# A routed expert stage on one core: the second accumulator folded into the output, the order of experts known sooner, and the smallest experts in the middle places

## The chip, the cores and the metric

The kernel runs on one core of one Trainium2 chip. The metric is the device time of one launch in microseconds (us). Lower is better.

## What is computed

One transformer layer over 2048 tokens of 256 numbers, in float32: a layer norm, attention with 16 heads (a band of 32 tokens back, and 16 global tokens), a residual, a second layer norm, and a feed-forward part that is the sum of two things: a shared SwiGLU over all tokens, and 64 experts of which each token uses 6. The change touches only the feed-forward part:

```python
scores = softmax(x @ gate_w.T)
topk_w, topk_idx = top_k(scores, 6)              # 64 experts, 6 per token
topk_w = topk_w / topk_w.sum(-1, keepdims=True)
# per expert e, for the tokens routed to it:
eo = (silu(buf @ w_gate[e].T) * (buf @ w_up[e].T)) @ w_down[e].T
y[token] += eo * topk_w                          # six additions per token
out = x1 + y + silu(x @ sh_gate.T) * (x @ sh_up.T) @ sh_down.T
```

`x1` is what attention and the residuals leave; it stays in SBUF in the tile `X1`, 16 blocks of 128 tokens.

## The kernel before, in words

**Attention and routing.** For every block of 128 tokens the kernel computes attention, then the router's choice, and GpSimd (POOL) scatters the block's rows with their six choices and weights into a DRAM array `expert_rows` by indirect DMAs, six of 128 rows per block (L1836). Meanwhile, TensorE (PE) goes on with the shared SwiGLU, two blocks at a time ("pairs" 0 to 4; pair_gate is L786, pair_up L797, pair_down L811). Blocks 0 and 1 are done earlier, and the last four blocks (NTL = 4, pairs 5 and 6) are left for after the experts.

**The order of the experts.** Between pairs 3 and 4 the counts per expert are turned into ranks on VectorE (DVE, function `ranks`). PE multiplies two small matrices by the one-hot rank matrix (L928, L929, at the head of pair 4), and DVE (`order`) writes `ids` (which expert stands in which place), `by_rank`, and `crowded` (how far an expert exceeds its room). The four experts 0 to 3 are FIXED in places 0 to 3; the other places follow by falling count. `HALF` (L73, from `LEVELS`, L71) gives for each place how many rows each of two tiles of this expert has: 128 for the first places, 72 for the last. `moved` rounds it up to a multiple of 16 for DMAs.

**The experts.** Each engine then runs 64 steps. For expert e: SP (SyncE) loads its rows, `XG` (L478), and its weights (L469 to L471: 368, 128 and 48 KB; 12 weight buffers, so 12 experts ahead, some of them in tiles that are free now: XB, zero, SMX, VW). PE transposes the rows (L947), multiplies (L960, L964), and multiplies down (L978, L981). ScalarE (ACT) does the SiLU (L1220, L1222) and scales the result into one of four `YE` buffers (L1233). DVE copies and multiplies (L1635, L1644, L1652) and computes from the rows each token's weight and address (`choices`, L1621 to L1625). POOL adds the two tiles of YE to DRAM by indirect DMAs with accumulation (L1850): even places into `acc_a`, odd ones into `acc_b`. The adds of place e wait until those of place e-2 have landed; ACT and DVE wait for those of place e-4 (YE has four buffers).

**Two programs.** If an expert is more crowded than its room, another version with loops runs (`full > 0`); the graded version that runs here stands in the `Else` on all five engines, and the closing part stands behind both.

**The end.** Once the adds are in, acc_a is loaded to SBUF in four quarters (L1903, POOL's queue), acc_b in four more (L566, SP's queue, after the last add has landed), both are added to X1 by DVE (L1690, L1697) and POOL (L1890, L1899), the shared SwiGLU of the last four blocks is added (pair_add, L1509), and SP stores out in four quarters (L569).

**SP's order before the experts:** wait `routed` (all rows scattered), load XG for places 0 to 3, wait `order_ready`, load the weights of places 4 to 11, read `crowded`, branch, and only then load XG for place 4 (L478 from L555).

Of the kernel before, what the change touches and what calls it, by code (L numbers as in the profile page):

```python
# [18 lines left out]

# [53 lines left out]
HALF = [P] * FIXED + [h for n, h in LEVELS for _ in range(n)]  # L73
# [40 lines left out]
def build(nc, x, glob, ln_s, ln_b, wq, wk, wv, wo, gate, w1, w2, shg, shu, shd, out):  # L114
    rows = nc.dram_tensor("expert_rows", (EX * CAP, ROW), F32, kind="Internal").ap()
    acc_a = nc.dram_tensor("acc_a", (T, D), F32, kind="Internal").ap()
    acc_b = nc.dram_tensor("acc_b", (T, D), F32, kind="Internal").ap()

    with ExitStack() as ctx:
# [61 lines left out]
        XA = SMX[:, :].rearrange("p (t d) -> p t d", t=NT)  # L181
# [29 lines left out]
        room = sb("room", [1, EX])  # L211
        count_e = sb("count_e", [EX, 1])
# [92 lines left out]
        a_ready, b_ready = sem("a_ready"), sem("b_ready")  # L305
# [10 lines left out]
        b_closed = sem("b_closed")  # L316
        a_in, b_in = sem2("a_in", 4), sem2("b_in", 4)
        a2_added = sem("a2_added")
        a_added, out_stored = sem("a_added"), sem("out_stored")
        sum_ready = sem2("sum_ready", 4)  # L320
# [106 lines left out]
        def quarter(v, q):  # L427
            return v[0:T, :].rearrange("(p t) d -> p t d", p=P)[:, q * NQ:(q + 1) * NQ, :]

        def held(v, q):  # L430
            return v[:, q * NQ:(q + 1) * NQ, :]
# [17 lines left out]
        def _(sp):  # L449
# [36 lines left out]
            def step(s):  # L486
# [14 lines left out]
                if s == 2 * LF:  # L501
                    for t in range(TPE):
                        sp.wait_ge(tile_zeroed[t], 16 * ZN)
                    sp.wait_ge(a_ready, 16)
                    sp.wait_ge(b_ready, 16)
# [15 lines left out]
            with sp.If(full > 0):  # L521
# [28 lines left out]
            with sp.Else():  # L550
                for p in range(EX - UN):
                    sp.wait_ge(et_done, p + 1)
                    sp.wait_ge(idx_ready, p + 1)
                    n = p + UN
                    expert_rows(expert(n), n % UN, 0, 2, HALF[n])  # L555
                    if p + AHEAD < EX:
                        sp.wait_ge(dn_done, p + 1)
                        weights(expert(p + AHEAD), p % AHEAD)

            def tokens(v, q):  # L560
                n = T // 4
                return v[q * n:(q + 1) * n, :].rearrange("(t p) d -> p t d", p=P)
# [7 lines left out]
            sp.wait_ge(out_stored, 16 * 4)  # L570
# [3 lines left out]
        def _(pe):  # L574
# [344 lines left out]
            for p in range(3, NPAIR):  # L919
# [5 lines left out]
                if p == 4:  # L925
# [4 lines left out]
                pair_gate(p)  # L930
                pair_up(p, pair_halves())
# [75 lines left out]
            with pe.If(full > 0):  # L1007
# [3 lines left out]
            with pe.Else():  # L1011
                experts(2, EX, graded_half)

            pair_gate(NPAIR)
            pair_up(NPAIR, pair_halves())
            pair_gate(NPAIR + 1)
            pair_down(NPAIR)
            pair_up(NPAIR + 1, pair_halves())
            pair_down(NPAIR + 1)
# [3 lines left out]
        def _(act):  # L1023
# [63 lines left out]
            def step(s):  # L1087
                a, b1, b2, c, d1, d2, e1 = (s - k for k in (0, LB, LP, LC, LD, LE, LE))
                if s == LF + 1:
                    na = T // P * D // 4  # L1090
                    act.wait_ge(zero_ready, 1)
                    for acc, done in ((acc_a, a_ready), (acc_b, b_ready)):
                        act.dma_start(acc.rearrange("(p n) d -> p (n d)", p=P).rearrange("p (n w) -> p n w", w=na),
                                     zero[:, 0:na].unsqueeze(1).broadcast_to([P, 4, na])).then_inc(done, 16)
# [163 lines left out]
            with act.If(full > 0):  # L1258
# [3 lines left out]
            with act.Else():  # L1262
                experts(2, EX, graded_half)

            for p in range(NPAIR, NPAIR + NTP):
                for h, fs in pair_halves():
                    act.wait_ge(g2_done, 2 * p + h + 1)
                    if p > NPAIR:
                        act.wait_ge(sh2_ready, 2 * (p - 1) + h + 1)
                    elif p > 0:  # L1270
                        act.wait_ge(sg2_ready, 2 * (p - 1) + h + 1)
                    act.activation(TH2[:, fs, :], pair_ps(0, h), ACT.Silu).then_inc(th2_ready, 1)
# [3 lines left out]
        def _(dve):  # L1276
# [291 lines left out]
            def ranks():  # L1568
# [12 lines left out]
                dve.tensor_scalar(at_rank[:, :], iota_e[0:EX, :], rank[:, 0:1], None, ALU.is_equal).then_inc(rank_ready, 1)  # L1581
# [97 lines left out]
            with dve.If(full > 0):  # L1679
                experts(2, EX, even_half)  # L1680
                experts(1, 2 * EX, even_half)
                dve.wait_ge(order_ready, 1)
            with dve.Else():
                experts(2, EX, graded_half)
# [275 lines left out]
```

## Time and profile before

| | us |
|---|---|
| median of 3 runs | 545.94 |
| lowest and highest | 545.63, 549.88 |
| the profiled execution, its own time | 546.38 |
| its span, from the first to the last instruction | 544.6 |
| mean granted TensorE clock, share of full speed | 0.97 |

The profiled execution is 1.8 us longer than its span, and 0.4 us above the median of the runs. The engines are PE (TensorE matmuls), PEld (its weight loads), DVE, ACT, POOL and SP; times in the rows are us from the span's start unless marked ns. The expert stage runs from about 245 to 521 us, and what comes after it until 544.6 us.

### The profile page before, as it was taken

The numbers are of one execution on the slowest core, as the hardware profiler recorded it, in microseconds if no ns is written. First come the engines' busy times: TensorE is split into PE (matmuls) and PEld (weight loads), VectorE is DVE, ScalarE is ACT, GpSimd is POOL, SyncE is SP. The second block draws the span as 40 slices with busy tenths as digits, with TensorE's granted clock in tenths as the row PEclk, the third lists the DMA queues.
The fourth block names the chain that finished last, engine by engine and source line by source line (L and its number), as shares of the span: only waits on it lengthen the run. The fifth ranks groups of instructions, "written<-read, shape, count | busy, mean of one in ns | idle before, by whom it ended". The sixth has DMA issues, their size and how long they took to land. (4 is left out here: it accounts for less than half of the span.)

```text
span 544.6 us, 13633 instructions
## 1 busy us (share of the span) xinstructions
PE 512.0 (94%) x4267; PEld 427.5 (78%) x4267; DVE 353.8 (65%) x1111; ACT 300.0 (55%) x899; POOL 340.0 (62%) x364
## 2 busy tenths in 40 slices
PE   8799999999999988989899999999999999999962
PEld 7698999999988877878577778877878787777651
DVE  3976888989999976745355555555555555555325
ACT  4797978999999851122244444444445454555300
POOL 4474254766566678701466766777777677678854
PEclk9898999899999979999899999999999999999996
DMA  8999999963222222257899999999999999965477
GB/s 288 393 383 389 400 397 389 332 238 105 89 100 99 100 84 102 104 184 231 212 231 231 233 250 242 238 250 254 236 238 252 244 244 244 237 119 84 48 219 261
DMA packets 67090, 122.16 MB, mean 224 GB/s; under 512 B 11296, under 2 KB 43872, under 8 KB 63936
## 3 DMA queue, kind: packets, MB, share of 16 engines
q0 software_dynamic: 24192, 54.81, 38.5%
q1 hardware_dynamic: 40672, 61.37, 36.4%
q10 hardware_dynamic: 2144, 5.00, 2.5%
q8 instruction: 37, 0.61, 0.5%
q14 instruction: 45, 0.37, 0.2%
HBM read 58.85 MB, written 60.23 MB: 219 GB/s over the span
## 5 line engine op out<-in xcount | busy, mean ns | idle before, releaser
L1850 POOL DMA_INDIRECT acc_a<-YE,dest x64 | 93.7, 1465 | 66.3 <-ACT YE L1233 32.9
L1836 POOL DMA_INDIRECT expert_rows<-XR,slot x96 | 95.6, 996 | 50.9 <-issue 27.8
L1850 POOL DMA_INDIRECT acc_b<-YE,dest x64 | 93.6, 1462 | 34.4 <-issue 19.0
L1233 ACT ACTIVATE YE<-PS,wsel 108x256 f32<-108x256 f32 (+14 forms) x128 | 53.5, 468 | 99.6 <-PE PS L981 99.6
L1059 ACT ACTIVATE SMX<-SMX,smax 128x112 f32<-128x112 f32 x256 | 75.0, 387 | 3.0 <-DVE smax L1459 3.0
L1644 DVE TENSOR_TENSOR HE<-SL,PS 128x216 f32<-128x216 f32 (+12 forms) x64 | 23.2, 362 | 81.3 <-ACT SL L1220 81.2
L1635 DVE COPY XET<-PS 128x432 f32<-128x432 f32 (+12 forms) x64 | 36.6, 574 | 24.0 <-PE PS L947 23.9
L960 PE MATMUL PS<-XET,W 128*128 128x256 f32 (+10 forms) x192 | 38.6, 344 | 0.0
L1445 DVE SCALAR_TENSOR_TENSOR SMX<-PS,mask 128x448 f32<-128x448 f32 x64 | 35.3, 613 | 3.8 <-PE PS L631 3.7
L960 PEld LDWEIGHTS PS<-XET,W 128*128 128x128 f32 x192 | 31.0, 189 | 8.6 <-issue 7.8
L698 PE MATMUL PS<-ident,SMX 128*112 128x128 f32 x240 | 35.1, 290 | 2.7 <-ACT SMX L1059 2.6
L1652 DVE TENSOR_TENSOR HE<-SL,PS 48x108 f32<-48x108 f32 (+14 forms) x128 | 33.4, 261 | 3.3 <-ACT SL L1222 0.4
L1068 ACT COPY PT<-PS 112x512 f32<-112x512 f32 x64 | 34.6, 592 | 1.6 <-PE PS L698 1.4
L1220 ACT ACTIVATE SL<-PS 128x216 f32<-128x216 f32 (+12 forms) x64 | 21.6, 337 | 24.6 <-PE PS L960 23.8
L947 PE MATMUL PS<-ident,XG 108*128 108x108 f32 (+13 forms) x256 | 32.4, 249 | 2.3 <-DMA XG<-expert_rows 2.3
L1459 DVE TENSOR_REDUCE smax<-SMX 128x8 f32<-128x896 f32 x32 | 33.1, 1073 | 0.0
L1222 ACT ACTIVATE SL<-PS 48x216 f32<-48x216 f32 (+12 forms) x64 | 21.2, 331 | 21.4 <-PE PS L964 21.3
L947 PEld LDWEIGHTS PS<-ident,XG 108*128 108x128 f32 (+13 forms) x256 | 28.9, 141 | 4.8 <-DMA XG<-expert_rows 2.7
L698 PEld LDWEIGHTS PS<-ident,SMX 128*112 128x112 f32 x240 | 28.0, 142 | 5.5 <-issue 3.0
L769 PE MATMUL PS<-VW,PT 112*64 112x17 f32 x960 | 30.9, 211 | 1.0 <-ACT PT L1068 1.0
L769 PEld LDWEIGHTS PS<-VW,PT 112*64 112x64 f32 x960 | 29.3, 138 | 2.9 <-ACT PT L1068 1.1
L631 PE MATMUL PS<-KW,QT 32*128 32x112 f32 x512 | 27.5, 281 | 0.2
(237 smaller groups left out, 1124.5 us busy)
## 6 DMA issues: line engine op xcount, KB each, us to landing
expert_rows<-zero POOLq DMA_DIRECT2D x24, 1088.0 KB, 14.1
W<-in_w SPq DMA_DIRECT2D x24, 368.0 KB, 3.8
XG<-expert_rows SPq DMA_DIRECT2D x24, 238.0 KB, 4.2
XB<-in_w SPq DMA_DIRECT2D x15, 368.0 KB, 3.6
SMX<-in_w SPq DMA_DIRECT2D x15, 368.0 KB, 3.7
XG<-expert_rows SPq DMA_DIRECT2D x24, 204.0 KB, 4.2
W<-in_w SPq DMA_DIRECT2D x24, 128.0 KB, 3.9
XG<-expert_rows SPq DMA_DIRECT2D x10, 272.0 KB, 3.7
```

The costliest lines, as they stand in the source:

```text
L698: mm = pe.transpose(PT_ps[:, n, k, :], SM[:, b2 % 2, NJ * n + k, :], ident[:, :])
L769: mm = pe.matmul(O_ps[q * BLK:(q + 1) * BLK, h, :], PT[0:NK, n, NB * k + q, e * BLK:(e + 1) * BLK], VW[0:NK, b2 % UN, q, h, :], start=True ...
L947: mm = pe.transpose(PS[:, e.odd, d * MAIN + t * h:d * MAIN + (t + 1) * h], XG[0:h, e.slot, t, d * P:(d + 1) * P], ident[0:h, 0:h])
L960: mm = pe.matmul(PS[:, 2 + q, u * MAIN:u * MAIN + n], W1S[j][:, d, u * P:(u + 1) * P], XET[:, q, d, 0:n], start=(d == 0), stop=(d == DC - 1))
L1059: i = act.activation(SM[:, b % 2, h], SM[:, b % 2, h], ACT.Exp, bias=smax[:, b % 2, h:h + 1])
L1068: act.copy(PT[0:NK, n], PT_ps[:, n]).then_inc(pt_evac, 1)
L1233: act.mul(YE[0:h, e.slot, t, :], PS[0:h, 5 + t, e.odd * D:(e.odd + 1) * D], wsel[0:h, e.slot, t:t + 1]).then_inc(y_ready, 1)
L1445: dve.scalar_tensor_tensor(out=sm, in0=sp_, scalar=SM_SCALE, in1=mk, op0=ALU.mult, op1=ALU.add).then_inc(s_read, 1)
L1635: dve.tensor_copy(XET[:, e.odd, :, 0:n], PS[:, e.odd, :].rearrange("p (c n) -> p c n", c=DC)[:, :, 0:n]).then_inc(et_evac, 1)
L1652: i = dve.tensor_tensor(HE[64 * t:64 * t + FT, q, 1, c], SL[0:FT, q, 1, c], PS[64:64 + FT, TAIL[q], c], ALU.mult)
L1836: pool.indirect_dma_start(rows, bass.IndirectOffsetOnAxis(ap=slot[:, d2 % UN, k:k + 1], axis=0), XR[:, d2 % UN, :], None, bounds_check=EX ...
L1850: pool.indirect_dma_start(target, bass.IndirectOffsetOnAxis(ap=dest[0:h, e.slot, t:t + 1], axis=0), YE[0:h, e.slot, t, :], None, bounds_ch ...
```

## The change

Five things are changed together.

- **The second array is folded.** `acc_a` is gone, and with it its zeroing (2 MB) and its four loads and additions. POOL writes X1 into `out` in three DMAs before the experts ("fills"), odd places accumulate straight into `out`, even places into `acc_b`. When all adds have landed, one DMA with accumulation adds the first twelve blocks of `acc_b` (1.5 MB) to `out` within DRAM. For the last four blocks SP loads `out` and `acc_b` (512 KB each), DVE adds them, adds the shared SwiGLU, and SP stores (256 KB twice).
- **The order is known sooner.** PE multiplies by the rank matrix behind pair_up(3) and not at the head of pair 4, DVE calls `order` right behind. SP waits for the order first, loads the weights of places 4 and 5, then XG of places 0 to 3, then the weights of places 6 to 9; the weights of places 10 and 11 come behind XG of places 4 and 5.
- **The branches are turned round.** The graded version stands in the `If`, the other one in the `Else`; PE, ACT and DVE have their closing part inside each branch.
- **The places are permuted.** Places 0 to 19 take ranks 0 to 19 (four fixed, sixteen largest), places 20 to 39 take the twenty smallest (ranks 44 to 63), places 40 to 63 the middle ones (ranks 20 to 43). HALF and `room` follow.
- **The closing part** on DVE no longer has additions between the two tail products.

```diff
-HALF = [P] * FIXED + [h for n, h in LEVELS for _ in range(n)]
+BY_RANK = [P] * FIXED + [h for n, h in LEVELS for _ in range(n)]
+RUNS = ((0, 20), (44, EX), (20, 44))
+RANKS = [r for first, end in RUNS for r in range(first, end)]
+HALF = [BY_RANK[r] for r in RANKS]
...
-        XA = SMX[:, :].rearrange("p (t d) -> p t d", t=NT)
+        XA = SMX[:, 0:NTL * D].rearrange("p (t d) -> p t d", t=NTL)
...
# SP
+            sp.wait_ge(pt_done, RG * NT)
+            sp.wait_ge(pv_done, RG * NT)
+            sp.wait_ge(order_ready, 1)
+            for j in range(FIXED, FIXED + 2):
+                weights(expert(j), j)
             sp.wait_ge(routed, 1)
             for j in range(UN):
                 expert_rows(j, j, 0, 2)
-            sp.wait_ge(order_ready, 1)
-            sp.wait_ge(pt_done, RG * NT)
-            sp.wait_ge(pv_done, RG * NT)
-            for j in range(FIXED, AHEAD):
+            for j in range(FIXED + 2, AHEAD - 2):
                 weights(expert(j), j)
             full = sp.value_load(crowded[0:1, 0:1], min_val=0, max_val=T)
-            with sp.If(full > 0):
+            with sp.If(full < 1):
+                for p in range(EX - UN):
+                    sp.wait_ge(et_done, p + 1)
+                    sp.wait_ge(idx_ready, p + 1)
+                    n = p + UN
+                    expert_rows(expert(n), n % UN, 0, 2, HALF[n])
+                    if p < 2:
+                        weights(expert(AHEAD - 2 + p), AHEAD - 2 + p)
+                    if p + AHEAD < EX:
+                        sp.wait_ge(dn_done, p + 1)
+                        weights(expert(p + AHEAD), p % AHEAD)
+            with sp.Else():
...
-            sp.wait_ge(b_closed, 1)
-            for q in range(4):
-                sp.dma_start(held(XB, q), quarter(acc_b, q)).then_inc(b_in[q], 16)
-            for q in range(4):
-                sp.wait_ge(sum_ready[q], 1)
-                sp.dma_start(tokens(out, q), held(X1, q)).then_inc(out_stored, 16)
+            sp.wait_ge(adds_closed, 1)
+            sp.dma_start(XA[:, :, :], tokens(out, NT - NTL, NTL)).then_inc(rest_loaded, 16)
+            sp.dma_start(XB[:, 0:NTL, :], tokens(acc_b, NT - NTL, NTL)).then_inc(rest_loaded, 16)
+            for k in range(NTP):
+                b = NT - NTL + 2 * k
+                sp.wait_ge(sh_add, b + 2)
+                sp.dma_start(tokens(out, b, 2), X1[:, b:b + 2, :]).then_inc(out_stored, 16)
...
# PE
-                if p == 4:
+                pair_gate(p)
+                pair_up(p, pair_halves())
+                if p == 3:
                     pe.wait_ge(rank_ready, 1)
                     pe.wait_ge(x2t_evac, NT)
                     pe.matmul(order_ps, expert_col[:, :], at_rank[:, :], start=True, stop=True)
                     pe.matmul(sorted_ps, count_e[:, :], at_rank[:, :], start=True, stop=True).then_inc(order_done, 1)
-                pair_gate(p)
-                pair_up(p, pair_halves())
...
# ACT: acc_a is no longer zeroed
-                    for acc, done in ((acc_a, a_ready), (acc_b, b_ready)):
-                        act.dma_start(...).then_inc(done, 16)
+                    act.dma_start(...).then_inc(b_ready, 16)
...
# DVE
-                dve.tensor_scalar(at_rank[:, :], iota_e[0:EX, :], rank[:, 0:1], None, ALU.is_equal).then_inc(rank_ready, 1)
+                dve.tensor_scalar(at_rank[:, :], rank_at[:, :], rank[:, 0:1], None, ALU.is_equal).then_inc(rank_ready, 1)
...
-                if p == 4:
+                pair_product(p)
+                if p == 3:
                     order()
-                pair_product(p)
                 pair_hidden(p)
...
+            def closing():
+                dve.wait_ge(d2_done, NPAIR)
+                tail_product(NPAIR)
+                tail_product(NPAIR + 1)
+                dve.wait_ge(rest_loaded, 32)
+                dve.wait_ge(out_filled, 16 * 3)
+                signal(dve.tensor_tensor(X1[:, NT - NTL:NT, :], XA[:, :, :], XB[:, 0:NTL, :], ALU.add), rest_summed, 1)
+                pair_add(NPAIR)
+                pair_add(NPAIR + 1)
+
+            with dve.If(full < 1):
+                experts(2, EX, graded_half)
+                closing()
...
# POOL
+            def fill(b, n):
+                pool.dma_start(tokens(out, b, n), X1[:, b:b + n, :]).then_inc(out_filled, 16)
+
+            pool.wait_ge(x1_ready, NT)
+            fill(NT - NTL, NTL)
+            pool.wait_ge(sh_add, 2 * NQ)
+            fill(0, 2 * NQ)
             pool.wait_ge(order_ready, 1)
             full = pool.value_load(crowded[0:1, 0:1], min_val=0, max_val=T)
...
-                added(e, acc_b if e.odd else acc_a, 2, h)
+                elif e.odd:
+                    pool.wait_ge(out_filled, 16 * 3)
+                added(e, out if e.odd else acc_b, 2, h)
...
+            pool.wait_ge(sh_add, 3 * NQ)
+            fill(2 * NQ, NQ)
             pool.wait_ge(b_ready, 16)
...
+            def fold():
+                def piece(v):
+                    return v[0:(NT - NTL) * P, :].rearrange("(p n) d -> p (n d)", p=P).rearrange("p (k w) -> p k w", w=4 * D)
+                pool.dma_start(piece(out), piece(acc_b), accum_op=ALU.add, max_dma_last_dim=4096).then_inc(folded, 16)
+
+            with pool.If(full < 1):
+                in_flight(pool, main_graded, False)
+            with pool.Else():
...
+            landed(2)
+            pool.sem_inc(adds_closed, 1)
+            fold()
+            pool.wait_ge(folded, 16)
```

## Rows read from the trace of the kernel before

**Rows 1.** Windows: length, busy per engine (instructions), granted clock, DMA share, GB/s

```profile
350.00:400.00 50.00, 50.00 (x296) 39.54 (x296) 27.63 (x99) 23.09 (x61) 35.39 (x24) 1.00 1.01 245
...
511.60:521.10 9.50, 9.50 (x46) 8.39 (x45) 1.11 (x2) 2.79 (x6) 7.93 (x6) 1.00 0.41 45
...
525.00:534.00 9.00, 4.26 (x12) 3.21 (x12) 5.67 (x8) 0.00 (x0) 3.21 (x2) 0.81 1.01 385
```

**Rows 2.** Timeline of PE over the first experts: start, duration, what, idle before

```profile
253.61 0.60 PE L947 MATMUL PS<-ident,XG 128*128 128x128 f32 x4
...
258.33 0.60 PE L947 MATMUL PS<-ident,XG 128*128 128x128 f32 x4
...
265.53 0.66 PE L947 MATMUL PS<-ident,XG 128*128 128x128 f32 x4 [2.32 <-DMA XG<-expert_rows]
...
271.90 0.59 PE L947 MATMUL PS<-ident,XG 124*128 124x124 f32 x4
```

**Rows 3.** Timeline of SP, 234 to 263 us

```profile
234.76 1.77 SPq L478 DMA_DIRECT2D XG<-expert_rows  x4
238.81 0.35 SPq L469 DMA_DIRECT2D XB<-in_w  x1
...
257.47 0.33 SPq L471 DMA_DIRECT2D VW<-in_w  x1
262.49 0.35 SPq L478 DMA_DIRECT2D XG<-expert_rows  x1
```

**Rows 4.** Timeline of all engines at the ordering, 229 to 246 us

```profile
229.32 2.75 PE L797 MATMUL PS<-X2T,shu_s 128*128 128x256 f32 x12
...
230.84 0.25 DVE L1581 TENSOR_SCALAR at_rank<-iota_e,rank 64x64 f32<-64x64 f32 x1
...
237.59 0.23 DVE L1591 COPY by_rank<-PS 128x64 f32<-128x64 f32 x1
...
242.26 2.46 PEld L811 LDWEIGHTS PS<-shd_s,SH 128*128 128x128 f32 x12 [2.07 <-issue]
```

**Rows 5.** Timeline from 509 us, all engines: the last expert and the end

```profile
509.97 1.05 PE L978 MATMUL PS<-W,HE 128*72 128x256 f32 x4 [1.02 <-ACT YE L1233]
...
511.66 0.83 ACT L1233 ACTIVATE YE<-PS,wsel 72x256 f32<-72x256 f32 x2 [1.83 <-PE PS L981]
...
517.92 1.42 POOL L1850 DMA_INDIRECT acc_b<-YE,dest  x1 [0.30 <-issue]
...
519.64 1.42 POOL L1850 DMA_INDIRECT acc_b<-YE,dest  x1 [0.30 <-DMA acc_a<-YE,dest]
...
522.01 2.75 PE L797 MATMUL PS<-X2T,shu_s 128*128 128x256 f32 x12
524.32 2.11 SPq L566 DMA_DIRECT2D XB<-acc_b  x4
525.92 1.23 DVE L1690 TENSOR_TENSOR X<-X,SMX 128x1024 f32<-128x1024 f32 x1 [8.40 <-DMA SMX<-acc_a]
...
529.65 4.26 PE L811 MATMUL PS<-shd_s,SG 128*128 128x256 f32 x12 [4.89 <-DVE SG L1704]
...
536.48 0.86 DVE L1509 SCALAR_TENSOR_TENSOR X<-PS,res_shift,X 128x256 f32<-128x256 f32 x2
536.59 3.66 SPq L569 DMA_DIRECT2D out<-X  x4
537.44 2.41 DVE L1697 TENSOR_TENSOR X<-X,XB 128x1024 f32<-128x1024 f32 x1
```

**Rows 6.** Timeline of PE: one step at 84 rows (places 51 to 57)

```profile
477.16 1.41 PE L960 MATMUL PS<-XET,zero 128*128 128x168 f32 x8
...
480.82 1.41 PE L960 MATMUL PS<-XET,SMX 128*128 128x168 f32 x8
```

**Rows 7.** DMA issues: what, count, KB each, median us from issue to landing

```profile
XG<-expert_rows SPq DMA_DIRECT2D x24, 238.0 KB, 4.2
...
out<-X SPq DMA_DIRECT2D x4, 512.0 KB, 4.0
```

More of the change, by code:

```diff
@@ L18 @@
 from contextlib import ExitStack
+from itertools import groupby
 import concourse.bass as bass
@@ L549, in _ @@
                 sp.wait_ge(order_ready, 1)
[L550 to L562, printed above, removed]
-            sp.wait_ge(b_closed, 1)
-            for q in range(4):
-                sp.dma_start(held(XB, q), quarter(acc_b, q)).then_inc(b_in[q], 16)
-            for q in range(4):
-                sp.wait_ge(sum_ready[q], 1)
-                sp.dma_start(tokens(out, q), held(X1, q)).then_inc(out_stored, 16)
-            sp.wait_ge(out_stored, 16 * 4)
+            sp.wait_ge(adds_closed, 1)
[5 more added lines that the diff above has]
+                sp.dma_start(tokens(out, b, 2), X1[:, b:b + 2, :]).then_inc(out_stored, 16)
+            sp.wait_ge(out_stored, 16 * NTP)
         @block.tensor
@@ L1005, in experts @@
                 in_flight(pe, step, half is even_half)
-            with pe.If(full > 0):
+            def closing():
+                pair_gate(NPAIR)
+                pair_up(NPAIR, pair_halves())
+                pair_gate(NPAIR + 1)
+                pair_down(NPAIR)
+                pair_up(NPAIR + 1, pair_halves())
+                pair_down(NPAIR + 1)
+            with pe.If(full < 1):
+                experts(2, EX, graded_half)
+                closing()
+            with pe.Else():
                 experts(2, EX, even_half)
@@ L1010, in _ @@
                 pe.wait_ge(order_ready, 1)
[L1011 to L1019, printed above, removed]
+                closing()
         @block.scalar
@@ L1256, in experts, with closing @@
                 in_flight(act, step, half is even_half)
-            with act.If(full > 0):
+            def closing():
+                for p in range(NPAIR, NPAIR + NTP):
+                    for h, fs in pair_halves():
+                        act.wait_ge(g2_done, 2 * p + h + 1)
+                        if p > NPAIR:
+                            act.wait_ge(sh2_ready, 2 * (p - 1) + h + 1)
+                        elif p > 0:
+                            act.wait_ge(sg2_ready, 2 * (p - 1) + h + 1)
+                        act.activation(TH2[:, fs, :], pair_ps(0, h), ACT.Silu).then_inc(th2_ready, 1)
+            with act.If(full < 1):
+                experts(2, EX, graded_half)
+                closing()
+            with act.Else():
                 experts(2, EX, even_half)
@@ L1261, in _ @@
                 act.wait_ge(order_ready, 1)
[L1262 to L1272, printed above, removed]
+                closing()
         @block.vector
@@ L1788, in order_constants @@
                 first = 0
-                for n, h in ((FIXED, P),) + LEVELS:
+                for h, run in groupby(HALF):
+                    n = len(list(run))
                     pool.memset(room[:, first:first + n], 2.0 * h)
+                    first += n
+                first = 0
+                for rank_0, end in RUNS:
+                    n = end - rank_0
+                    pool.iota(rank_at[:, first:first + n], pattern=[[1, n]], base=rank_0, channel_multiplier=0,
+                              allow_small_or_imprecise_dtypes=True)
                     first += n
@@ L1901, in load_a @@
-            def load_a():
-                for q in range(4):
-                    pool.dma_start(held(XA, q), quarter(acc_a, q)).then_inc(a_in[q], 16)
-            with pool.If(full > 0):
+            def fold():
[4 more added lines that the diff above has]
+                in_flight(pool, main_graded, False)
```

104 lines of the change are left out of this document (24 added, 80 removed).

## The prediction

> **What bounds the kernel now.** I read the windows first, then PE's timeline where a window was not full, and last the end in all engines. From 270 us until the last expert PE is busy all the time: 50.00 of 50 us, at the full granted clock, while POOL is at 35 and the DMA engines at a share of 1.01 with 245 GB/s [rows 1]. So PE's own work sets the pace of the experts, with the DMA engines and POOL's adds close behind it. I call E the moment when PE has finished the last expert's down product; ACT starts on it at 511.66 [rows 5], so E = 511.6. Two stretches are not PE's work. One is a hole at the fourth transposition: L947 comes every 4.72 us (253.61, 258.33), then at 265.53, with 2.32 us of waiting for XG, and the next only at 271.90, since matmuls run long meanwhile [rows 2]. The other is all that follows E: 33.0 us until the span's end, in which PE works some 16 us and nobody needs PE for most of it. There the chain is: POOL starts the last place's adds at 517.92, 6.3 us behind E; its second at 519.64; SP may load acc_b at 524.32; XB arrives, DVE adds until 539.85, the last quarter goes out and lands at 544 [rows 5].
>
> **Before E, part by part.**
>
> *The order of experts and the turned branch.* The ranks are there at 231.09, pair_up(3) of PE ends at 232.07, and the order is out only at 237.82, since its matmuls stand behind pair_down(2) and its DVE part waits for them [rows 4]. Put behind pair_up(3), with 0.6 us of matmuls and 1.3 us of DVE work, it is out at about 234.0. That alone gives PE nothing: PE is busy with pairs, and the 0.6 us only change places. What PE can win is the 2.07 us without work at 242.26, which the profile puts down to issue, right where it reads `crowded` and goes into the `Else` [rows 4]. In the new version the graded code follows directly and the value is 4 us old, so most of it goes. But XG of place 0 now stands behind two sets of weights: SP takes 19.0 us for 8 sets, 2.4 each, and 1.0 us from the order to the first one [rows 3, 4]; so 235.0 + 4.8 = 239.8 and not 234.76, and with 4.2 us of landing [rows 7] 244.0. PE wants it behind pair_down(3), at 242.26 - 2.07 + 2.8 = 243.0 [rows 4]. A new stall of 0.9 us takes its part back. I take -1.2; the ends are -2.1 (XG in time) and +1.0 (POOL's fills, 1.5 MB in the same stretch, delay XG by another 2 us: 1.5 MB are 4 us at 385 GB/s [rows 1], half of it in front of XG).
>
> *XG of place 4.* SP is done with weights at 257.8 and issues XG for place 4 at 262.49 [rows 3], although what it waits for there is long done; the 4.7 us between them are its way through reading `crowded` and the branch. With two sets fewer ahead of it and the branch falling through it is issued near 252 (239.8, 1.8 for the four XG, four sets of 2.4, 0.8), ten us sooner. The hole goes whole: 7.20 - 4.72 = 2.5 us of wait and 6.37 - 4.72 = 1.6 us of the slow clock behind it [rows 2], together -4.1. No other step of SP is late afterwards: it needs 3 to 4 us per place, PE 4.7, and the weights of places 10 and 11 are wanted 45 us later. The end below is -3, if a rest of the wait stays.
>
> *Places.* The same 64 sizes are computed, so PE's own sum stays. At the end of before POOL needs 1.72 us per add of two [rows 5], 3.44 per place, and PE is at less than that for the last three; with POOL 6 us behind, PE waits 1.02 us for YE [rows 5]. With 92 to 96 rows at the end PE needs 3.9 per place, and this wait goes: -1.0. Against it, the twenty smallest now run with weight loads beside them (they had almost none). A step of 84 rows is 3.66 us [rows 6]. I put +1 on it, between 0 and +9 (the second rival).
>
> *No zeroing of acc_a, the fills' issue, rank_at, more memsets:* beside PE's work in stages where PE is full; 0. The last fill goes out behind pair_add(4), before the first YE exists, and only the odd places wait for it.
>
> E is then 511.6 - 1.2 - 4.1 - 1.0 + 1.0 = 506.3.
>
> **Behind E.** POOL now closes with places of PE's pace over its own (3.9 against 3.46), so its lag shrinks from 6.3 to about 2 us. The last add starts at E + 3.7, and the step from there to "landed" is that of before, 519.64 to 524.32, 4.7 us [rows 5]: E + 8.4. POOL has a jump to make first, over the other version; SP's pause of 4.7 us with its read [rows 3] is the nearest row, and most of it lies beside the landing. I put 0.6: adds_closed at E + 9.0 = 515.3 (before: E + 12.7).
>
> From there two chains run side by side. *The last four blocks:* two loads of 512 KB beside the fold, 7 us (4.0 is the landing of a 512 KB DMA [rows 7], and the fold shares the engines): 522.3; one DVE addition of 1.3 [rows 5], two pair_adds of 0.9 each [rows 5]: 525.4. The products and pair_down(6) are long done, as DVE no longer stands in front of them: PE's L797 ends 13.2 us behind E, and down takes 2.8 at full clock, so E + 17 = 523.3. The last store of 256 KB lands within 4.0 [rows 7]: 529.4, and the program is over 0.6 later: 530.0. *The fold:* 1.57 MB. The trace has no direct accumulating DMA. The indirect adds move 45 GB/s at a share of 0.41 [rows 1], so 110 GB/s with full engines, 14.3 us; a plain transfer runs at 385 GB/s [rows 1], 4.1 us. The pieces are 4 KB against 1 KB, so I take 10 between the two, the 1.5 MB beside it included; with 1.2 to issue and 2.6 for the landing and the end: 529.1. The last blocks end it by a hair. What was late before (five additions of 1.2 to 2.8 us on two engines, and four stores of 512 KB, which had to wait for them) is gone.
>
> SP takes 4.7 us for its branch here [rows 3]. The Trainium skill (Runtime: NRT & Kernel Launch, section Instruction fetch mechanics) says that a taken branch to a target outside the two-page window has to fetch that page by DMA before the engine can go on. The trace agrees for SP. By that rule POOL pays a fetch after its last add, since the version that it jumps over is long: at SP's price 1.1 us over the landing, where I put 0.6; the sum would be 532.0.
>
> **The sum.** The span is 530.0; the profiled execution lies 1.8 over its span, 531.8, and 0.4 over the median of the runs: 531.4, rounded 531.5. Of the 14.4 us, 5.3 come before E and 9 behind it.
>
> **The rivals.**
>
> 1. *The fold ends it.* At the adds' own rate, 14.3 us, and 4 for the 1.5 MB beside it: 515.3 + 1.2 + 18.3 + 2.6 = 537.4, so 538.8. For it: it is the only rate that the trace shows for an accumulating DMA; against it: rows of 1 KB at scattered addresses. Chance 0.18.
> 2. *The small places become a DMA chain.* An add waits for those two places back: 1.73 to the second one, 0.3, and its landing; 4.7 us at the end with idle engines [rows 5], and by my estimate 5.2 beside the weights; so 3.6 us per place, just under the 3.66 of PE [rows 6]. With 1 us more landing beside the weights (the share is 1.01 already [rows 1]) it is 4.1, and 20 places cost 9 us: 540. Against it: at 92 and 96 rows before, with the same bytes, PE stood nowhere. Chance 0.12.
> 3. *The lag stays.* POOL ends as far behind as before: +4, 535.5. Chance 0.08.
> 4. *Slower: the fold crawls.* It is bound by latency and not by bytes, and gets no more than the 45 GB/s that the adds show outright [rows 1]: 35 us, 515.3 + 1.2 + 35 + 2.6 = 554, so 555.5. It decides from 25.5 us on, below 62 GB/s. Against it: those adds leave the engines free for 0.59 of the time. Chance 0.04.
> 5. *The change doesn't do what it says:* with the places permuted a room doesn't fit, the looped version runs, and 64 more places come on top: over 650. All of rank, room and HALF are permuted alike. Chance 0.01.
>
> **How the numbers follow.** The forecast has 0.57: 526 to 535 by itself (fold and loads at their fast ends: -5; the loss at XG and the branch: +3). A measurement of this kernel tells about 1% from no change. Faster by over 1%, below 540.5: the forecast, rival 3, nearly all of rival 1 and half of rival 2, 0.90; within 1%: 0.05; slower by over 1%: 0.05. The range of 525 to 540 holds the forecast and the centres of rivals 1 to 3.
>
> **What would show it.** In the changed profile: no idle PE beyond 1 us between 240 and 275, and a clock of 1.00 there; by_rank at 234; XG of place 4 issued before 255; steps of 3.7 at 84 rows; the last add within 3 us of E plus its own 3.2; E near 506; adds_closed at 515; the fold landing within 14 us of its issue. I am wrong if PE's idle time moves into places 20 to 39, or if POOL's wait for the fold is the last thing and lasts beyond 20 us.

## The result and the profile after

| | before | after |
|---|---|---|
| median, us | 547.91 (545.63 to 551.66, 4 runs) | 540.77 (538.63 to 547.45, 4 runs) |
| the profiled execution, us | 546.38 | 540.55 |
| its span, us | 544.6 | 538.8 |
| granted TensorE clock | 0.97 | 0.979 |

The kernel before has a fourth run here, of 551.66 us. The ratio is 0.986, with an interval of 0.981 to 0.991: faster by 1.4%. It leaves out the run of 547.45, in which the chip was in a slower state. The forecast was 531.5, with a range of 525 to 540; the sign was right, but only about half of the expected gain came (7.1 us by the medians, of 14.4), and 540.77 lies above the range.

Three stretches carry it. "Start" runs from the beginning of pair_down(3) on PE to the first L960; before, it begins with the hole of 2.07 us that stands ahead of pair_down(3), at 240.19. E is the end of the last down product, as in the prediction.

| us | before | after | change | predicted |
|---|---|---|---|---|
| start: pair_down(3) to the first L960 | 8.24 | 10.62 | +2.4 | -1.2 |
| first L960 to E | 263.19 | 261.26 | -1.9 | -4.1 |
| E to the end of the span | 32.98 | 26.64 | -6.3 | -9.3 |

The three misses are 3.6, 2.2 and 3.0, together 8.8: the span that was predicted was 530.0. Each has its own cause.

The windows after, which answer to [rows 1]. PE is still full among the large places, at the granted clock of 1.00. The second line covers the fold, the third a part of it in which neither SP's loads nor its stores run: 205 GB/s.

```profile
350.00:400.00 50.00, 50.00 (x330) 38.31 (x330) 27.75 (x108) 25.06 (x68) 35.73 (x26) 1.00 1.00 248
...
522.60:535.30 12.70, 5.57 (x25) 4.25 (x23) 4.08 (x7) 0.00 (x0) 1.08 (x1) 0.90 1.02 244
...
526.00:528.00 2.00, 2.00 (x10) 1.77 (x11) 1.95 (x3) 0.00 (x0) 0.00 (x0) 1.00 1.04 205
```

All engines at the ordering, which answers to [rows 4]. The order is out at 233.82 instead of 237.82, within 0.2 us of what the prediction said.

```profile
230.68 0.25 DVE L1588 TENSOR_SCALAR at_rank<-rank_at,rank 64x64 f32<-64x64 f32 x1
...
231.84 0.43 PE L930 MATMUL PS<-at_rank,expert_col 64*128 64x64 f32 x2
...
233.59 0.23 DVE L1598 COPY by_rank<-PS 128x64 f32<-128x64 f32 x1
```

PE from pair_down(3) on. Its L811 at 240.28 starts without a gap: the hole of 2.07 us is gone. But behind it PE stands for 2.67 us until XG is there, and the transposes and the next L811 run long: 1.68 us and 3.89 us (1.04 and 2.75 in e1, below).

```profile
240.28 2.75 PE L811 MATMUL PS<-shd_s,SH 128*128 128x256 f32 x12
245.70 1.68 PE L947 MATMUL PS<-ident,XG 128*128 128x128 f32 x8 [2.67 <-DMA XG<-expert_rows]
247.17 3.89 PE L811 MATMUL PS<-shd_s,SG 128*128 128x256 f32 x12
250.90 1.89 PE L960 MATMUL PS<-XET,W 128*128 128x256 f32 x8
...
256.08 0.60 PE L947 MATMUL PS<-ident,XG 128*128 128x128 f32 x4
```

What makes them long is the clock. It was granted at 1.00 before the wait and through it. When PE works again, a part of the time goes by at the lower of TensorE's two levels: the windows show 0.62 and 0.70 (the number before the DMA share), and 1.00 again from 251 us on. In the profile before, 0.62 and 0.86 stood behind the 2.32 us of waiting of [rows 2], and 1.00 behind the hole of 2.07.

```profile
245.70:247.20 1.50, 1.50 (x9) 1.33 (x10) 0.69 (x1) 0.00 (x0) 0.00 (x0) 0.62 1.03 401
247.20:251.00 3.80, 3.80 (x14) 3.17 (x14) 1.48 (x3) 0.00 (x0) 0.00 (x0) 0.70 0.93 280
```

SP in the same stretch, which answers to [rows 3]. XG is issued 4.24 us later than before, behind two sets of weights, and its four issues take 4.45 us where they took 1.77. XG of place 4 goes out at 255.33 instead of 262.49.

```profile
234.88 0.38 SPq L468 DMA_DIRECT2D XB<-in_w  x1
...
239.00 4.45 SPq L477 DMA_DIRECT2D XG<-expert_rows  x4
...
251.87 1.36 SPq L470 DMA_DIRECT2D SMX<-in_w  x1
255.33 0.35 SPq L477 DMA_DIRECT2D XG<-expert_rows  x1
```

From the places with 76 and 72 rows, all engines without the weight loads of PE. DVE finds the token addresses of a place (L1628 to L1632) only when the adds that used the same slot four places back have landed; it stands 2.13 us for them. Behind this on DVE's queue are HE (L1651) and XET (L1642), the rows that PE multiplies next; XET is ready at 411.94, and PE's L960 starts at 412.05, after 0.78 us of idle time that the profile puts down to issue.

```profile
409.65 1.03 PE L978 MATMUL PS<-W,HE 128*76 128x256 f32 x4
410.30 0.23 DVE L1628 SCALAR_TENSOR_TENSOR hit<-XG,by_rank 80x12 f32<-80x12 f32 x1 [2.13 <-DMA acc_b<-YE,dest]
...
411.14 0.30 DVE L1651 TENSOR_TENSOR HE<-SL,PS 128x144 f32<-128x144 f32 x1
...
411.36 0.58 DVE L1642 COPY XET<-PS 128x416 f32<-128x416 f32 x1
...
412.05 1.65 PE L960 MATMUL PS<-XET,XB 128*128 128x208 f32 x8 [0.78 <-issue]
```

The waits of DVE in sum: what was waited for, us in total, times, longest. In the profile before, the same instruction waited 4.7 us for acc_b and 4.1 for acc_a. Most of the 40 us cost PE nothing: its holes behind issue are 1.9 us in all.

```profile
DVE hit L1628 <- DMA acc_b<-YE,dest: 21.9, 13, 2.7
...
DVE hit L1628 <- DMA out<-YE,dest: 18.2, 14, 2.9
```

The end, all engines, which answers to [rows 5]. The last down product ends at 512.16. POOL begins the last place at 515.31, the second add at 517.05; SP loads at 520.59, and the fold goes out at 522.62.

```profile
510.49 1.07 PE L978 MATMUL PS<-W,HE 128*92 128x256 f32 x4 [1.02 <-ACT YE L1236]
511.49 0.67 PE L981 MATMUL PS<-W,HE 48*92 48x256 f32 x4
...
515.31 1.43 POOL L1861 DMA_INDIRECT out<-YE,dest  x1 [0.30 <-issue]
...
517.05 1.43 POOL L1861 DMA_INDIRECT out<-YE,dest  x1 [0.30 <-issue]
...
520.59 0.42 SPq L564 DMA_DIRECT2D SMX<-out  x1
...
522.62 1.08 POOL L1900 DMA_DIRECT2D out<-acc_b  x1 [4.14 <-issue]
...
525.85 1.23 DVE L1700 TENSOR_TENSOR X<-SMX,XB 128x1024 f32<-128x1024 f32 x1
...
528.01 2.06 SPq L569 DMA_DIRECT2D out<-X  x2
```

The DMA issues that answer to [rows 7]: KB each and the median us to landing. The fold takes 12.7 us for 1.5 MB.

```profile
out<-acc_b POOLq DMA_DIRECT2D x1, 1536.0 KB, 12.7
```

And SP's last waits, with the DRAIN at the end of POOL's queue (its duration in ns, then its start). The fold lands at 535.36 and the second store at 536.50, 1.1 us behind it. But POOL, which has waited for the fold, has a DRAIN of 3.02 us to do from 535.54 on, and only after this the program ends, another 2.1 us behind the stores. From the fold's landing to the end it takes 3.4 us.

```profile
SPq L122 <- DMA out<-X: 6.4, 1, 6.4
...
SPq L122 <- PEq L122: 2.1, 1, 2.1
...
L122 POOLq DRAIN  x1: 3017/3017/3017, 535.5 to 535.5; - x1
```

### The profile page after: what moved, and what is told of

Its sections match the earlier page's. It is cut to its first block, busy times and chain, and to the rows that moved or that the text cites. A ratio compares the mean times of both kernels' runs of the same rounds, so it can differ in the third digit from the quotient of the medians.

```text
span 538.8 us, 13623 instructions
## 1 busy us (share of the span) xinstructions
PE 509.7 (95%) x4267; PEld 425.6 (79%) x4267; DVE 345.0 (64%) x1107; ACT 299.8 (56%) x899; POOL 334.1 (62%) x365
## 4 chain that ended last, share of the span: by engine, by line
PE 55%; issue 1%; DMA 1%; DVE 1%; SPq 1%; ACT 0%; DVEq 0%
PE PS L960 18%; PE PS L978 10%; PE PS L964 8%; PE PS L981 7%; PE PS L947 4%; PE PS L811 3%; PE PS L797 2%; PE PS L786 1%; DMA XG<-expert_rows 1%; SPq L483 0%; SPq L470 0%; SPq L469 0%; SPq L468 0%; ACT YE L1236 0%; DVE hot L1410 0%
## 5 line engine op out<-in xcount | busy, mean ns | idle before, releaser
L1861 POOL DMA_INDIRECT out<-YE,dest x64 | 93.6, 1462 | 34.2 <-issue 13.3
L1236 ACT ACTIVATE YE<-PS,wsel 104x256 f32<-104x256 f32 (+14 forms) x128 | 53.5, 468 | 96.0 <-PE PS L981 96.0
L1651 DVE TENSOR_TENSOR HE<-SL,PS 128x216 f32<-128x216 f32 (+12 forms) x64 | 23.2, 362 | 56.1 <-ACT SL L1223 55.4
L1642 DVE COPY XET<-PS 128x432 f32<-128x432 f32 (+12 forms) x64 | 36.6, 572 | 18.8 <-PE PS L947 18.4
L1628 DVE SCALAR_TENSOR_TENSOR hit<-XG,by_rank 112x12 f32<-112x12 f32 (+3 forms) x64 | 14.6, 228 | 41.3 <-DMA acc_b<-YE,dest 21.9
L960 PE MATMUL PS<-XET,W 128*128 128x256 f32 (+9 forms) x192 | 38.3, 342 | 0.3 <-issue 0.2
L960 PEld LDWEIGHTS PS<-XET,W 128*128 128x128 f32 x192 | 30.8, 189 | 8.9 <-issue 8.2
L1659 DVE TENSOR_TENSOR HE<-SL,PS 48x104 f32<-48x104 f32 (+14 forms) x128 | 33.4, 261 | 3.5 <-ACT SL L1225 0.7
L947 PE MATMUL PS<-ident,XG 108*128 108x108 f32 (+12 forms) x256 | 33.0, 252 | 2.7 <-DMA XG<-expert_rows 2.7
L947 PEld LDWEIGHTS PS<-ident,XG 108*128 108x128 f32 (+12 forms) x256 | 29.2, 142 | 5.3 <-issue 3.0
```

Source lines behind the costliest of these rows:

```text
L947: mm = pe.transpose(PS[:, e.odd, d * MAIN + t * h:d * MAIN + (t + 1) * h], XG[0:h, e.slot, t, d * P:(d + 1) * P], ident[0:h, 0:h])
L960: mm = pe.matmul(PS[:, 2 + q, u * MAIN:u * MAIN + n], W1S[j][:, d, u * P:(u + 1) * P], XET[:, q, d, 0:n], start=(d == 0), stop=(d == DC - 1))
L1236: act.mul(YE[0:h, e.slot, t, :], PS[0:h, 5 + t, e.odd * D:(e.odd + 1) * D], wsel[0:h, e.slot, t:t + 1]).then_inc(y_ready, 1)
L1642: dve.tensor_copy(XET[:, e.odd, :, 0:n], PS[:, e.odd, :].rearrange("p (c n) -> p c n", c=DC)[:, :, 0:n]).then_inc(et_evac, 1)
L1861: pool.indirect_dma_start(target, bass.IndirectOffsetOnAxis(ap=dest[0:h, e.slot, t:t + 1], axis=0), YE[0:h, e.slot, t, :], None, bounds_ch ...
```

## The experiments

In the first two groups (e1 to e4, e5 to e8) the stage of attention and routing took some 90 us longer in every kernel, the one before included (medians of 645.46 and 640.75). So stages are compared, and medians only within a group. In the third group (e9 to e11) the kernel before had 549.06.

### e1: XG first in SP's queue

```diff
-            sp.wait_ge(order_ready, 1)
-            for j in range(FIXED, FIXED + 2):
-                weights(expert(j), j)
             sp.wait_ge(routed, 1)
             for j in range(UN):
                 expert_rows(j, j, 0, 2)
-            for j in range(FIXED + 2, AHEAD - 2):
+            sp.wait_ge(order_ready, 1)
+            for j in range(FIXED, AHEAD - 2):
```

> The changed kernel, but SP issues XG of places 0 to 3 as soon as the rows are scattered, and only then waits for the order and loads the weights of places 4 to 9. Theory (the place in SP's queue made XG late: it went out from 239.0 to 243.5 us instead of 234.8 to 236.5): PE no longer waits 2.67 us for XG before its first L947 and its matmuls run at full clock there; place 0's first L960 starts near 247.3 instead of 250.9, and the time falls by 3 to 4 us. Rival (the 1.5 MB of fills, new in this stretch, are what delays it): XG still lands near 244, the gain is below 1 us.

Measured: 639.82 us, a ratio to before of 0.992 (0.989 to 0.996). The start took 6.06 us (340.56 to 346.62), against 10.62 after and 11.2 to 13.2 in the five later profiles that keep the weights first (12.55 and 13.2 in e2 and e3). The unaltered kernel wasn't run in this group, so the forecast of 3 to 4 us in time isn't tested here. The next lines are PE's in e1: the transposes follow without a wait and at full clock.

```profile
340.56 2.75 PE L809 MATMUL PS<-shd_s,SH 128*128 128x256 f32 x12
343.15 1.04 PE L945 MATMUL PS<-ident,XG 128*128 128x128 f32 x8
344.03 2.75 PE L809 MATMUL PS<-shd_s,SG 128*128 128x256 f32 x12
```

So XG's late issue costs 4.6 us of the profile after: 2.67 of waiting, 1.7 of matmuls that run long behind it (the transposes and L811 take 1.47 and 3.73 us from start to start, 0.88 and 2.59 in e1), and 0.2 ahead of it. The rival isn't ruled out by this: in e1 XG goes out at 334.92, ahead of the weights but also of both fills (335.69 and 338.21), and after it went out behind the fills (235.42 and 237.92). The six profiles with the weights first hint that the fills count. Where the fill of 1 MB was issued 1.1, 1.9, 2.3, 2.9, 3.1 and 4.5 us ahead of XG (after, e2, e4, e8, e5, e3), PE's first transposition came 6.7, 6.6, 6.1, 5.3, 5.7 and 4.2 us behind XG's issue.

### e2: places by falling rank

```diff
-RUNS = ((0, 20), (44, EX), (20, 44))
+RUNS = ((0, EX),)
```

> The changed kernel with the places in falling order, as before (ranks 0 to 63 in places 0 to 63). Theory (the permutation moves the adds' lag away from the end, but pays for it with holes in PE's middle, 1.9 us in all): the holes of PE between 405 and 480 us go, so PE's last down ends 1.5 to 2 us sooner, but POOL's last add starts 6 us behind it instead of 3.2 before it is in the stage's last place: the time rises by 1 to 2 us. Rival (the holes are no work of the order of places but of the adds into two arrays at a full DMA load): they stay somewhere, and the time rises by 3 us or more.

Measured: 641.28 us, ratio 0.992 (0.989 to 0.995). First L960 to E: 259.56, against 261.26 after and 264.24 in e1; of the holes on PE behind issue one of 0.47 is left. E to the end: 30.81, against 26.64 and 27.04, as POOL's last add starts 7.8 us behind E and not 4.9. What the permutation takes from the end, it costs before E. In time, e2 has the same ratio to before as e1.

### e3: POOL's closing inside its branch

`landed(2)`, `sem_inc(adds_closed)`, the fold and its wait are moved from behind the branches into each of them:

```diff
             with pool.If(full < 1):
                 in_flight(pool, main_graded, False)
+                landed(2)
+                pool.sem_inc(adds_closed, 1)
+                fold()
+                pool.wait_ge(folded, 16)
```

> The changed kernel, but on POOL the waits for the last adds, adds_closed and the fold stand inside the graded branch (and again in the other), so that POOL jumps over the other version only after the fold. Theory (the 4.1 us between the last add and the fold's issue hold a jump of some 2 us beyond the landing): the fold is issued about 2 us sooner relative to the last add, and the time falls by 1.5 to 2.5 us. Rival (they are landing and the DMA's own preparation): less than 0.5 us. If the jump is only moved behind the fold, the span's end would keep it: the fold sooner, but the time unchanged.

Measured: 644.23 us, ratio 1.001 (0.997 to 1.004), the slowest changed kernel of its group. From the last add to SP's load it took 3.52 us (3.54 after), and 2.0 us more to the fold, as after: there was nothing to win. SP's last wait grew:

```profile
SPq L122 <- DMA out<-X: 7.7, 1, 7.7
...
SPq L122 <- PEq L122: 4.7, 1, 4.7
...
L122 POOLq DRAIN  x1: 3082/3082/3082, 638.2 to 638.2; - x1
```

The fold landed at 635.66, and POOL's DRAIN began 2.6 us behind that, against 0.2 us in the profile after. From the fold's landing to the end it took 5.9 us, against 3.4 to 3.6 in every other profile with a fold. So the jump over the other version costs 2.5 us where nothing covers it. In the changed kernel it lies beside the landing of the last adds; here it follows the fold, at the very end. The theory fell. E to the end was 30.63; the rest of the 4.0 us over the profile after is a fold that took 1.1 us longer and a last add that started 0.4 us later.

### e4: no fold

`fold()` and the wait for it are left out, so the first twelve blocks lack what the even places add.

> The changed kernel without the fold: the first twelve blocks of acc_b are never added to out. Theory (fold and last stores share the DMA engines to the end, so the fold sets both: the stores land 6.8 us after issue because of it): the stores land in about 3 us, the end comes 3.5 to 5 us sooner. Rival (the end is set by PE's last down and the stores, the fold is hidden beside it): less than 1.5 us.

Measured: 636.18 us, ratio 0.985 (0.978 to 0.992). E to the end: 21.78, against 26.64 after. The 256 KB stores land in 3.3 us instead of 6.8, and SP's last wait behind them is 0.2:

```profile
SPq L122 <- DMA out<-X: 3.4, 1, 3.4
```

The fold is on the path and costs 4.9 us there: 3 of them as the stores wait for their share of the DMA engines, and 1.9 because POOL's DRAIN stands behind the fold. Without the fold POOL begins its DRAIN at 619.9; it takes 7.9 us there, and is over before SP issues its first store at 628.02.

### e5: the changed kernel again, beside e6 to e8

> The changed kernel, unaltered, as the measure for the other runs of this call. From its first L960 to the end of the last down 261 to 264 us, from there to the span's end 26.5 to 27 us. Theory (the price of small places beside weight loads): its holes in PE lie in places 30 to 41 and behind place 50, 2 to 4.5 us in all. Rival (they are chance): they lie elsewhere than in e1, e3 and e4.

Measured: 638.78 us (632.78 to 648.11), ratio to before 0.994 (0.990 to 0.999). First L960 to E 262.30, with holes of 0.31 to 0.96 and 1.02 at the last down; E to the end 27.36; the fold 13.6. The holes before the last lie in places 39, 47, 50, 53 and 55, 2.8 us in all, one of them (0.96) a wait for XG; those of e1, e3 and e4 lie in 32 to 41 and 51 to 55. So the sum came as the theory said, the places only roughly.

### e6: XG first, large and small places by turns

```diff
-RUNS = ((0, 20), (44, EX), (20, 44))
-RANKS = [r for first, end in RUNS for r in range(first, end)]
+RANKS = list(range(FIXED)) + [r for k in range((EX - FIXED) // 2) for r in (FIXED + k, EX - 1 - k)]
```

On top of e1's edit; the iota and the memsets of `room` follow.

> The changed kernel with XG of places 0 to 3 first in SP's queue (as in e1) and another order of places: four fixed, then largest, smallest, second largest, second smallest and so on, so that the middle sizes come last. Theory (a run of small places beside weight loads is what lets the adds fall behind until DVE and PE wait): with each small place beside a large one the holes in PE go but for the 1.0 at the last down, first L960 to last down takes about 259.5 us, the last add starts within 3.5 us of it, and the time is 5 to 8 us below the changed kernel's: 4.5 for XG, 2 to 3 for the places. Rival (the DMA load of the whole stage is what counts, not its order): the holes stay at 2 us or more, only e1's gain is there.

Measured: 631.16 us (629.45 to 635.19), ratio 0.987 (0.979 to 0.994), the fastest of its group; the interval overlaps that of e5. But not by holes that had gone: first L960 to E was 264.03, with nine holes of 0.16 to 0.67 behind issue and a wait of 1.05 for XG of place 6. The holes stay even when no two small places follow one another directly.

### e7: the kernel before with only the branches turned

On all five engines the graded version goes into the `If`; the closing part of PE, ACT and DVE goes into each branch.

> The kernel before with only its branches turned round on all engines (graded version in the If, closing parts inside on PE, ACT and DVE). Theory (the way into the Else cost PE 1.7 to 2.1 us and SP 4.7): PE's 2.07 us without work before pair_down(3) goes, SP issues XG of place 4 within 1.5 us of its last weights instead of 5 and PE's wait of 2.3 us and the slow clock behind it go: the time falls by 4 to 6 us. Rival (the wait at place 4 was due to eight sets of weights ahead in SP's queue): a part of it stays, and the gain is 2 us.

Measured: 638.39 us, ratio 0.995 (0.992 to 0.999). The hole of 2.07 us ahead of pair_down(3) is gone. SP issues XG of place 4 1.7 us behind its last weights, and not 4.7 us as in [rows 3]. First L960 to E: 260.61 instead of 263.19. The wait for XG of place 4 shrank but stayed, and nothing ran long behind it (the clock stays at 1.00): the next L947 comes 4.78 us later, where it came 6.37 later before [rows 2].

```profile
352.46 0.66 PE L947 MATMUL PS<-ident,XG 128*128 128x128 f32 x4 [1.33 <-DMA XG<-expert_rows]
357.24 0.59 PE L947 MATMUL PS<-ident,XG 124*128 124x124 f32 x4
```

The branch alone gives 2.6 of the 4.1 us at place 4, besides the hole of 2.07; the rest is put down to the two sets of weights that went behind XG of place 4, and wasn't run by itself. The gain in time, 2.4 us by the medians, is nearer to the rival's 2 us than to the theory's 4 to 6. The end took 36.24 here instead of 32.98, with loads and stores that landed later (acc_b 9.8 us instead of 8.6); whether that is the chip's or the edit's stays open.

### e8: the fold written in pieces of 1 KB

```diff
-rearrange("p (k w) -> p k w", w=4 * D)
+rearrange("p (k w) -> p k w", w=D)
```

> The changed kernel with the fold cut into pieces of 1 KB instead of 4 KB, the same bytes. Theory (the fold's price is by the piece, as in the adds, which are 1 KB): it takes up to 14 us or more to land where it took 12.7 to 13.8. Rival (the price is by the byte): it lands after the same 12.7 to 14 us.

Measured, in one run: 636.75 us. The fold landed in

```profile
out<-acc_b POOLq DMA_DIRECT2D x1, 1536.0 KB, 14.5
```

against 12.1 to 14.0 in the nine other profiles with a fold. But the edit changed the text of the kernel and not the transfer. POOL's queue moved just as many packets as in e5, the unaltered kernel:

```profile
q0 software_dynamic: 24576, 56.39, 34.4%
```

In e4, without the fold, it is 24176. So the fold is 400 packets for its 1.57 MB in e8 too, some 4 KB each, and e8 is one more run of the changed kernel. Theory and rival are both untested: whether the fold's price goes by the piece or by the byte stays open. The Trainium skill (Perfetto Trace Analysis, section DMA Optimizations) says that DMAs under 2 KB carry significant overhead each, and that batching small transfers into larger ones can improve the throughput dramatically; no run here shows it for this transfer, or against it.

### e9, e10, e11: three orders of the places, with XG in time

All have e1's edit. e9 keeps the permutation, e10 has falling ranks (e2's edit), e11 is e6 again.

> The changed kernel with XG of places 0 to 3 first in SP's queue, as in e1, now beside the two others of this call. Theory (the sixteen largest together, then the twenty smallest together, cost PE stalls before E and save the end behind it): first L960 to E 264, span minus E 27. Rival (the 264 of e1 was its run's own): 261.5, as in the changed kernel's first profile.

> As e9, but the places by falling rank as in the kernel before. This is the worth of the permutation with XG in time. Theory (worth nearly nothing net): first L960 to E 259.5, 4 us shorter than in e9; span minus E 31, 4 us longer; the total within 1.5 us of e9. Rival (the permutation pays, as predicted): total 4 us above e9. Second rival (it costs): total 3 us or more below e9.

> As e9, but large and small places by turns, as in e6. Theory (small places do not stand 20 in a row, but the last places are middle ones and a place of few rows still waits for the adds now and then): first L960 to E 263 to 264, span minus E 26, total 0 to 2 us below e9. Rival (the 631 of e6 came from the interleaving): total 5 us or more below e9.

| us | e9, permuted | e10, falling | e11, by turns |
|---|---|---|---|
| median of 4 | 540.13 | 539.58 | 538.07 |
| ratio to before | 0.985 (0.979 to 0.990) | 0.983 (0.977 to 0.989) | 0.980 (0.974 to 0.986) |
| start | 6.05 | 6.06 | 6.05 |
| first L960 to E | 262.61 | 259.64 | 263.43 |
| E to the end | 25.96 | 30.04 | 26.30 |

The windows of PE over the places with the fewest rows of e9, and of the same time in e10 (which has larger places there): 46.70 of 50 us busy against 50.00. Behind the first L960, e10 has no hole behind issue at all, e9 has five (3.3 us) in places 35 to 43, e11 five (2.4 us). A wait for XG of place 6 stands in e10 (0.37 us) and e11 (1.43), and not in e9.

```profile
380.00:430.00 50.00, 46.70 (x298) 35.69 (x297) 24.08 (x97) 23.26 (x63) 34.70 (x25) 1.00 0.95 234
```

```profile
380.00:430.00 50.00, 50.00 (x307) 39.68 (x305) 26.61 (x99) 24.13 (x65) 35.57 (x26) 1.00 0.99 244
```

And DVE's waits for the adds in e10, an eighth of those of e9 (23.5 and 23.0):

```profile
DVE hit L1626 <- DMA out<-YE,dest: 4.0, 6, 1.3
...
DVE hit L1626 <- DMA acc_b<-YE,dest: 2.0, 4, 0.7
```

The permutation is worth nothing that can be measured here: e9 lies 0.1% above e10, and the intervals reach some 0.6% to each side. It moves 3 to 4 us from behind E to before E. The three orders can't be told apart by their medians. Nor does the start that is 4.6 us shorter show in the ratios: e9 has 0.985, the changed kernel 0.986 in its own group. e11 has the lowest median, 2.0% below before, and is the version to take; that it beats e9 by its order of places isn't shown.

## Why the prediction failed, by its steps

**What bounds the kernel** held among the large places: PE is full in [rows 1] and in the same window after. The stretches that it named as no work of PE's (the 2.07 us ahead of pair_down(3), the hole at place 4, and what follows E) were the right ones; new ones opened among the small places.

**The order of experts and the turned branch** failed in the size of one term, and with its sign. The order came 4.0 us sooner, the hole of 2.07 went, PE wanted XG at 245.70 - 2.67 = 243.0, as predicted, and SP issued it at 239.00 (239.8 predicted). "With 4.2 us of landing" was the step that failed. That is the median of 24 issues at a time when SP sends one at a time; here the four issues take 4.45 us instead of 1.77, right behind two sets of weights and two fills on POOL's queue, and PE starts 6.7 us behind the first issue. The stall was 2.67 and not 0.9, and it cost another 1.7 us, since the clock fell behind it (0.62 and 0.70). The prediction had read this second cost in [rows 2], 1.6 us behind 2.32 of waiting, and counted it where it disappears, but not where a new stall of the same length could appear. The text had the fills as a bound of +1.0; the change came to +2.4. e1 shows the whole price, 4.6 us. How it divides between the weights and the fills wasn't tried; the six profiles set side by side under e1 speak for a part of the fills.

**XG of place 4** was nearly right: the hole and the long matmuls behind it went. It was issued at 255.33 and not near 252, since the four XG issues took 4.45 us and not 1.8, and the pause behind the weights was 2.1 us and not 0.8; it was still in time. By PE's L981 of place 3 (273.29 before, 271.63 after), 2.4 of loss at the start and 4.1 of gain leave -1.7. e7 adds that turning the branches alone gives 2.6.

**Places.** "With 92 to 96 rows at the end this wait goes: -1.0" was wrong. The wait of 1.02 for YE stands in every run, with 72, 92 or 96 rows in the last place (1.02 or 1.03). It is no sign of POOL's lag. PE has no other product between the last two downs, so it waits here for ACT to empty the accumulator of the place before (0.83 us from 509.51 on, right behind PE's L981). The +1 for small places was 1.9 after (holes of 0.24, 0.78, 0.16 and 0.74, in places 39, 40, 46 and 55), and 2.8 to 4.5 in the other profiles with the permutation, mostly in places 32 to 41. The prediction had named idle time of PE in places 20 to 39 as a sign that it is wrong. Rival 2 had the right place and cause, the landing of adds of earlier places, which doesn't shrink with the rows: beside the weight loads it took 5.2 us with 84 rows and 5.2 with 108, and 3.4 with 96 rows in places 57 and 61, where no weights are loaded any more. Its +9 was far too much. What it missed is the way: not POOL, but DVE stands for the adds, with PE's operands behind it in its queue.

E is then 511.62 - 1.9 + 2.4 = 512.1, where 506.3 was predicted.

**Behind E.** The lag is 3.2 us (515.31 - 512.16), half of before's 6.3, but not 2; the last add starts at E + 4.9, where E + 3.7 was predicted. adds_closed came at E + 8.4, against E + 9.0, since from there it took 3.5 us and not 4.7 + 0.6: two errors that nearly cancel, which is luck. The 4.7 was no landing with idle engines, as rival 2 calls it: before, POOL's four loads of acc_a went out 1.9 us behind the last add, and nothing of that kind runs beside it now. The jump was hidden, as taken. e3 shows 2.5 us for it without cover. The Trainium skill (Runtime: NRT & Kernel Launch, section Instruction fetch mechanics) has a taken branch out of the window wait for a fetch of its target page; the prediction's estimate by that rule, 1.1 us over the landing, didn't come, as from the last add to SP's load it took as long in e3, without a jump there, as after.

Behind adds_closed come 2.0 us to the fold (1.2 predicted), 12.7 for the fold (10) and 3.4 from its landing to the end (2.6), of which POOL's DRAIN is 3.0: E + 26.6. The term of the fold was mis-sized most. It was to hold the other 1.5 MB too. By the 205 GB/s of the fold alone, 1.57 MB are 7.7 us, and the loads and stores beside it 4.1 us at 385 GB/s [rows 1]: an estimate of 11.8. Rival 1, "the fold ends it", was the right mechanism, at 12.7 us and not 18.3, as the fold alone moves nearly twice the 110 GB/s of the indirect adds. The prediction had the stores end it by a hair. They take 6.8 us beside the fold instead of 4.0 and land 1.1 us behind it. In e4 the program ends 0.4 us behind its last store; here POOL's DRAIN behind the fold holds the end 1.9 us longer. The four misses, -0.6, +0.8, +2.7 and +0.8, make 3.8 before rounding over the fold's chain as predicted, E + 22.8, and so 3.0 over the forecast's 23.7.

## What to carry to other kernels

A stall that a change may create costs what such a stall cost in the old trace, the long matmuls behind it included: whoever books that gain at one place must book the price at the other. Before a load that the bounding engine is about to need, no other transfers are started; the weights and fills that went out ahead of XG were wanted tens of us later, and cost 4.6. Small steps put in the middle drain the last engine's lag at the end only by what they cost in the middle, when each step waits for adds whose landing doesn't shrink with the rows. At the end, look also at what the engine that awaits the last DMA has still to do: here POOL's DRAIN of 3.0 us begins only then. Whether another engine's wait for the fold would save it wasn't run. Whether an edit of the kernel's text changes a transfer is read from its packets; that of e8 didn't.

## What was not expected of the hardware

A direct accumulating DMA within DRAM moves 1.5 MB in 12.1 to 14.5 us beside 1.5 MB of loads and stores. In the 2 us in which it has the engines for itself it moves 205 GB/s in the profile after, at a share of 1.04, and 191 to 211 in e2, e5, e8 and e9. That is between the 110 GB/s that the indirect adds of [rows 1] would give with full engines, by their share, and the 385 of plain loads. The 256 KB stores beside it land in 6.3 to 7.9 us (medians) instead of 3.3. Between SP's first load behind adds_closed and the issue of the fold, on the engine that gave the signal, lie 2.0 us in every run with a fold. And POOL's DRAIN at the end takes 2.9 to 3.2 us behind a fold, and 7.9 us when it comes right behind the last adds.
